# The second attention with transposed scores, three rotating pairs of score banks, and one unit weighed per slot

## The chip, the cores and the metric

The kernel runs on one core of a Trainium2 chip, in one launch. The metric is the time of that launch on the device, in microseconds; the median of three runs is given. Profiled executions are compared by their span, from the first to the last instruction of the core.

## The reference, cut to what matters

The kernel computes two layers in a row on an image batch of 2 x 256 channels x 32 x 32, in fp32. The first is a deformable attention with a bias network and an MLP; nothing in it is recomputed otherwise by the change. The second is plain self-attention over 1024 positions with 8 heads of 32 channels:

```python
xf = transpose(x.reshape(B, C, N), (0, 2, 1))          # B=2, C=256, N=1024
qkv = (xf @ W_qkv + b_qkv).reshape(B, N, 8, 96)
q, k, v = split(qkv, 3, axis=-1)
attn = einsum('bihd,bjhd->bijh', q, k) * 32 ** -0.5
attn = softmax(attn, axis=2)                           # over j, the keys
res = einsum('bijh,bjhd->bihd', attn, v).reshape(B, N, 256)
x = transpose(res @ W_out + b_out + xf)                # back to B, C, 32, 32
```

There are 16 pairs of batch and head (G), and the kernel calls each a head.

## The kernel before, in words

Five engines run written-out instruction orders and wait for one another by counting semaphores. SP issues nearly all DMAs, in order. Up to the end of the first layer's MLP (about 1026 us) the change touches only where some small tiles lie and one wait of SP.

**V, Q and K.** TensorE first computes V for 16 blocks of 128 positions (L1026: two products of 128x256 each, fp32), and VectorE adds the bias (L741). Then eight units compute Q and K, alternately, for 128 channels x 1024 positions (L1038: four products of 128x512). An fp32 product shows in the profile as two records. ScalarE writes the high part in fp32r (L531), VectorE the remainder (L767), and SP stores both to DRAM (`q_d`, `k_d`, L299). Between these, VectorE splits V into three bf16 parts.

**The attention loop.** A head's Q and K come back from DRAM as a stack: four copies of 32 rows, high and low parts paired so that one fp32r product of 128 rows sums high x high, high x low, low x high and low x low. Each of 16 heads has 8 units of 128 queries. For a unit, TensorE makes the scores 128 queries x 1024 keys in two matmuls (L1047). VectorE reduces them to the negated maximum (L773), ScalarE takes the exponential with it as bias (L535), and TensorE turns the result in eight 128x128 transposes (L1055). The turned probabilities are split into fp16 high and low parts: ScalarE copies out of PSUM (L540, L543), VectorE casts and subtracts (L776, L779), GpSimd subtracts the other half (L390). TensorE then weighs them with V in sixteen matmuls of 97 columns (L1063), the 97th being the sum. VectorE inverts the sum (L786), ScalarE scales (L550), and GpSimd adds the three parts (L395, L397). The loop is rolled, two heads in a turn. Two pairs of PSUM banks hold scores, one pair the turned values, one pair the outputs.

**The end.** 32 transposes (L1102) and copies (L574) bring the result to channels x positions, eight units of two 128x512 products apply the output weights (L1113), VectorE adds bias and input (L814), and SP stores (L327).

`bank(i, n)` is n banks of PSUM from bank i; NK = 8; HALF = 512.

## Time and profile before

| | us |
|---|---|
| median of 3 runs (lowest, highest) | 1402.49 (1401.10, 1406.26) |
| the profiled execution's own time | 1401.21 |
| its span | 1399.0 |
| V, Q and K (first L1026 to last L1038) | 1027.1 to 1068.7 |
| attention (first L1047 to last L1063) | 1073.9 to 1375.8 |
| final transposes, products, stores | 1378.3 to 1399.0 |

| engine | busy us of the span | share |
|---|---|---|
| PE (TensorE matmul) | 1302.2 | 93% |
| PEld (its weight loads) | 616.0 | 44% |
| DVE (VectorE) | 921.5 | 66% |
| ACT (ScalarE) | 967.6 | 69% |
| POOL (GpSimd) | 748.9 | 54% |

The shares are averages over stages with different limits; the first attention's bias network alone takes some 760 us. A matmul's recorded length includes its way through the array, so matmuls overlap in the records, and the distance from start to start tells more than the length. "Idle before" of a group is what its engine waited ahead of it.

### The profile page before, as it was taken

The page shows a single profiled execution, that of the slowest core. Times are in us where ns is not written, and L with a number is a line of the kernel's source. Part 1 is how long each engine was busy: PE and PEld are TensorE (multiplying, and loading weights), DVE is VectorE, ACT ScalarE, POOL GpSimd, SP SyncE. Part 2 cuts the span into 40 slices and gives each one's busy share as a digit, 9 for nine tenths or more (in the row PEclk, how much of TensorE's full clock was granted, in tenths as well). Part 3 has the DMA queues.
Part 4 walks back from the last instruction along what each step waited for, and adds up shares of the span by engine and source line. Part 5 has one row for each costly group of instructions (what it writes and reads, how often), then busy time and mean ns, then how long its engine had stood idle before and what let it go on. Part 6 is the DMA issues. An engine that isn't in the chain of part 4 may idle for free.

```text
span 1399.0 us, 29958 instructions
## 1 busy us (share of the span) xinstructions
PE 1302.2 (93%) x11666; PEld 616.0 (44%) x11666; DVE 921.5 (66%) x1270; ACT 967.6 (69%) x1263; POOL 748.9 (54%) x681
## 2 busy tenths in 40 slices
PE   3169999999999999999999998799997999999998
PEld 2132222222222222222222226444454888888885
DVE  6876666666666666666666657410037999999995
ACT  3377777777777777777777773332204999999994
POOL 4166666666666666666666652200000767777772
PEclk9579999999999999999999999999999999999999
DMA  2141110111011101110111000000007222212211
GB/s 69 54 134 31 31 32 2 31 31 32 2 31 32 29 4 32 31 26 7 31 32 23 9 1 1 1 0 0 0 29 272 62 60 60 54 45 52 60 30 60
DMA packets 19922, 53.27 MB, mean 38 GB/s; under 512 B 4642, under 2 KB 7330, under 8 KB 19668
## 3 DMA queue, kind: packets, MB, share of 16 engines
q1 hardware_dynamic: 19824, 51.92, 14.1%
q8 instruction: 70, 1.15, 0.4%
q14 instruction: 24, 0.20, 0.0%
q10 hardware_dynamic: 4, 0.01, 0.0%
HBM read 40.95 MB, written 10.95 MB: 37 GB/s over the span
## 4 chain that ended last, share of the span: by engine, by line
PE 80%; DVE 11%; issue 3%; ACT 2%; POOL 2%; DMA 1%; SPq 1%; DVEq 0%; ACTq 0%; POOLq 0%
PE ps L898 31%; PE ps L907 17%; PE ps L889 5%; DVE aneg L773 5%; PE ps L1055 4%; PE ps L1063 4%; PE ps L1004 4%; PE ps L1014 4%; PE ps L1047 3%; DVE conv L620 2%; PE ps L1038 1%; DVE big L776 1%; POOL big L355 1%; PE ps L1026 1%; PE ps L991 1%
## 5 line engine op out<-in xcount | busy, mean ns | idle before, releaser
L898 PE MATMUL ps<-big,w 64*64 64x512 f32 x4096 | 483.5, 589 | 0.0
L479 ACT ACTIVATE big<-ps 128x1024 f32<-128x1024 f32 x256 | 262.0, 1023 | 179.0 <-PE ps L898 179.0
L674 DVE TENSOR_SCALAR big<-big 128x1024 f32<-128x1024 f32 x256 | 177.8, 694 | 263.8 <-POOL big L370 263.8
L668 DVE TENSOR_TENSOR big<-qpad,ps 128x1024 f32<-128x1024 f32 x256 | 311.0, 1215 | 7.8 <-ACT ps L458 5.4
L370 POOL TENSOR_TENSOR big<-qpad 128x1024 f32<-128x1024 f32 x128 | 244.5, 1910 | 133.2 <-PE ps L898 68.6
L370 POOL TENSOR_TENSOR big<-qpad,V 128x1024 f32<-128x1024 f32 x128 | 244.5, 1910 | 129.7 <-PE ps L898 73.5
L479 ACT ACTIVATE big<-ps,vec 128x1024 f32<-128x1024 f32 x256 | 284.0, 1109 | 0.0
L390 POOL TENSOR_TENSOR big<-BT,big 128x512 f16<-128x512 f32 x129 | 150.4, 1166 | 248.0 <-DVE big L776 248.0
L907 PE MATMUL ps<-big,w3s 128*32 128x512 f32 x2048 | 246.2, 598 | 1.3 <-ACT big L479 1.3
L898 PEld LDWEIGHTS ps<-big,w 64*64 64x64 f32 x4096 | 146.6, 133 | 205.9 <-issue 112.6
L773 DVE TENSOR_REDUCE aneg<-ps 128x1 f32<-128x1024 f32 x131 | 158.3, 1209 | 6.0 <-PE ps L1047 5.7
L535 ACT ACTIVATE big<-ps,aneg 128x1024 f32<-128x1024 f32 x130 | 148.5, 1142 | 6.0 <-DVE aneg L773 5.3
L1055 PE MATMUL ps<-ident,big 128*128 128x128 f32 x1032 | 136.3, 274 | 3.8 <-DVE big L779 3.8
L907 PEld LDWEIGHTS ps<-big,w3s 128*32 128x32 f32 x2048 | 53.5, 109 | 181.7 <-ACT big L479 92.2
L1055 PEld LDWEIGHTS ps<-ident,big 128*128 128x128 f32 x1032 | 121.1, 141 | 23.2 <-DVE big L779 5.7
L1063 PE MATMUL ps<-BT,big 128*128 x2048 | 115.6, 208 | 1.1
L1063 PEld LDWEIGHTS ps<-BT,big 128*128 128x128 f16 x2048 | 99.0, 97 | 21.3 <-issue 10.3
L889 PE MATMUL ps<-S,wl 57*64 57x512 bf16 x1024 | 102.3, 389 | 1.5 <-ACT vs L474 1.5
L1047 PE MATMUL ps<-h1l,h1h 128*128 128x512 f32 x262 | 94.5, 443 | 6.8 <-DMA h1l<-k_d 5.2
L889 PEld LDWEIGHTS ps<-S,wl 57*64 57x64 bf16 x1024 | 29.5, 105 | 144.7 <-ACT big L479 80.7
L779 DVE SCALAR_TENSOR_TENSOR big<-ps,big 128x512 f16<-128x512 f32 x129 | 89.1, 691 | 0.8 <-ACT big L543 0.4
L540 ACT ACTIVATE BT<-ps 128x512 f32<-128x512 f32 x129 | 79.1, 613 | 4.0 <-PE ps L1055 4.0
(140 smaller groups left out, 1116.5 us busy)
## 6 DMA issues: line engine op xcount, KB each, us to landing
raw<-s_f SPq DMA_DIRECT2D x32, 512.0 KB, 6.1
h1h<-q_d SPq DMA_DIRECT2D x64, 128.0 KB, 3.0
h1l<-k_d SPq DMA_DIRECT2D x64, 128.0 KB, 3.1
q_d<-XN SPq DMA_DIRECT2D x8, 512.0 KB, 2.6
k_d<-XN SPq DMA_DIRECT2D x8, 512.0 KB, 2.6
X<-in_x SPq DMA_DIRECT2D x2, 1024.0 KB, 6.3
out<-X SPq DMA_DIRECT2D x8, 256.0 KB, 2.0
m<-grid_d SPq DMA_DIRECT2D x1, 1024.0 KB, 4.6
```

The costliest lines, as they stand in the source:

```text
L370: pool.tensor_tensor(h1[m % HRING].rearrange("p (y a b) -> p y a b", y=2, b=W), u.unsqueeze(2).to_broadcast(shape), a[:, :, HALF // W * hf ...
L390: pool.tensor_tensor(PTL[u % 2][:, 0:HALF], PF[u % 2], PTH[u % 2][:, 0:HALF], ALU.subtract).then_inc(pFl_ready, 1)
L479: act.activation(h2[m % H2RING], z2[m % ZRING], ACT.Relu, bias=v("cb2") if m % 2 else 0.0).then_inc(h2_ready, 1)
L535: act.activation(PR[u % 2], bank(2 * (u % 2), 2), ACT.Exp, bias=aneg[u % 2][:, :]).then_inc(pr_ready, 1)
L668: dve.tensor_tensor(h1[m % HRING].rearrange("p (y a b) -> p y a b", y=2, b=W), u.unsqueeze(2).to_broadcast(shape), b[:, :, HALF // W * hf: ...
L674: dve.tensor_scalar(h1[m % HRING], h1[m % HRING], 0.0, None, ALU.max).then_inc(h1_ready, 1)
L773: dve.tensor_reduce(aneg[u % 2][:, :], bank(2 * (u % 2), 2), AX.X, ALU.max, negate=True).then_inc(mx_ready, 1)
L889: pe.matmul(z2[m % ZRING][CH * y:CH * (y + 1), HALF * x:HALF * (x + 1)], wl1[CH * x:CH * x + KROWS, 2 * w + y, :], S[CH * x:CH * x + KROWS ...
L898: last = pe.matmul(z2[m % ZRING][CH * y:CH * (y + 1), HALF * x:HALF * (x + 1)], w2[CH * x:CH * (x + 1), :], h1[m % HRING][CH * x:CH * (x + ...
L907: last = pe.matmul(zb[32 * k:32 * (k + 1), :], w3s[:, a:a + 32], h2[(m + k // 2) % H2RING][:, HALF * (k % 2):HALF * (k % 2 + 1)], start=(m ...
L1055: last = pe.transpose(bank(4 + hf)[:, P * i:P * (i + 1)], PR[u % 2][:, P * jt:P * (jt + 1)], ident[:, :])
L1063: last = pe.matmul(bank(6 + u % 2)[:, 0:VW], pT[u % 2][:, P * jt:P * (jt + 1)], V3[:, 2 * k + u // NK, jt, :], start=(jt == order[0] and p ...
```

## The change

The second attention is written anew.

- V is computed after Q and K. Its bias comes as a third product, of a row of ones with the bias row, and ScalarE copies V out of PSUM.
- The stack has three copies of 32 rows (96) instead of four. Three heads' stacks are held; the first three are loaded after four of the eight units of Q and K are stored, before the rest is.
- The scores are made twice. `along(x)` makes 128 queries x 1024 keys, for which every eighth query is taken as the stationary operand, so only VectorE reads them, for the maxima (`maxes`). `across(s)` makes 128 keys x 1024 queries, with two more rows: a row pair of ones against the high and low parts of the negated maxima, which subtracts them in the product. ScalarE's exponential writes the probabilities already turned, in fp32.
- The maxima travel from 128 partitions x 8 to two rows of 1024: GpSimd splits them (`max_parts`), SP writes them to DRAM and reads them back (`move_max`).
- A slot has one `along` (13 ahead), one `across`, and one `weigh` of two slots before: four matmuls of 256 queries, V (32 columns) being stationary, in four column tiles. For the sum, GpSimd adds the probabilities of two slots, and every second slot four matmuls with ones (`sums`) add them over the partitions. Outputs and sums are 32 rows per quarter of the queries.
- Once per head VectorE inverts the sums and multiplies (`divide`), and SP moves the four quarters into place (`place_head`), so that the final transposes go.
- Scores use three pairs of banks in rotation. All loops are unrolled.
- `conv`, `gel`, `qw` and `kw` of the first layer share memory with other tiles now, and SP waits for `k_ready` ahead of the late weights.

```diff
-Q_STACK, K_STACK = [0, 0, 1, 1], [0, 1, 0, 1]
-VW = 3 * D + 1
-PSCALE = 2.0 ** 12
+Q_STACK, K_STACK = [0, 0, 1], [0, 1, 0]
+ROWS = D * len(Q_STACK)
+HEADS3, PRING, AHEAD_MAX = 3, 6, 13
+QUARTER = N // 4
 WS_POOL = 4
-UNITS = 2 * NK
+SLOTS = G * NK
...
+        PT = [big[:, 4 + i, :] for i in range(PRING)]
+        PSUMS = [big[:, 11, :], BT[:, 14:16, :].rearrange("p a b -> p (a b)")]
+        OT = [big[:, 10, QUARTER * i:QUARTER * (i + 1)] for i in range(2)]
+        orec = [big[:, 10, QUARTER * i:QUARTER * (i + 1)] for i in (2, 3)]
...
+        def along_banks(x):
+            return 2 * (x % 2 if x < AHEAD_MAX else 2 * (x - AHEAD_MAX) % 3)
+        def across_banks(s):
+            return 2 * ((2 * s + 1) % 3)
...
+            sp.wait_ge(k_ready, 1)
...
+            def load_head(n):
+                i = n % HEADS3
+                for r in range(len(Q_STACK)):
+                    sp.dma_start(QS[i][D * r:D * (r + 1), :].bitcast(fp32), q_d[Q_STACK[r], D * n:D * (n + 1), :]).then_inc(st_in[i], 16)
+                    sp.dma_start(KS[i][D * r:D * (r + 1), :].bitcast(fp32), k_d[K_STACK[r], D * n:D * (n + 1), :]).then_inc(st_in[i], 16)
+            def move_max(n):
+                sp.wait_ge(m_lo, n + 1)
+                sp.dma_start(m_d[n].rearrange("a (q t) -> q a t", t=NK), mparts[n % HEADS3][:, :, :].bitcast(fp32)).then_inc(m_out, 16)
+                sp.wait_ge(m_out, 16 * (n + 1))
+                sp.dma_start(QS[n % HEADS3][ROWS:ROWS + 2, :].bitcast(fp32), m_d[n]).then_inc(m_in, 16)
+            def place_head(n):
+                sp.wait_ge(o_done, n + 1)
+                row, t = D * (n % HP), n // HP
+                for c in range(4):
+                    sp.dma_start(rT[row:row + D, t, QUARTER * c:QUARTER * (c + 1)], OT[n % 2][D * c:D * (c + 1), :]).then_inc(rT_in[n % 2], 16)
+            for n in range(4):
                 send_parts(n)
             for i in range(2):
-                sp.wait_ge(parts_out[i], 32 * 3)
-            load_head(0, 0)
-            load_head(1, 1)
-            for n in range(6, 2 * T):
+                sp.wait_ge(parts_out[i], 32 * 2)
+            for n in range(HEADS3):
+                load_head(n)
+            for n in range(4, 2 * T):
                 send_parts(n)
             for i in range(2):
                 sp.wait_ge(parts_out[i], 32 * T)
-            with sp.Fori(0, G // 2 - 1) as k:
-                sp.wait_ge(sc_ready, UNITS * k + NK)
-                load_head(0, 2 * k + 2)
-                sp.wait_ge(sc_ready, UNITS * k + 2 * NK)
-                load_head(1, 2 * k + 3)
-            sp.wait_ge(sc_ready, UNITS * (G // 2 - 1) + NK)
-            sp.sem_inc(st_in[0], 16 * 2 * HP)
+            for n in range(G):
+                move_max(n)
+                if n >= 2:
+                    place_head(n - 2)
+                if HEADS3 <= n + 2 < G:
+                    sp.wait_ge(st_ready, NK * (n + 2 - HEADS3 + 1))
+                    load_head(n + 2)
+            place_head(G - 2)
+            place_head(G - 1)
...
+            def max_parts(n):
+                pool.wait_ge(mx_ready, NK * (n + 1))
+                if n >= HEADS3:
+                    pool.wait_ge(m_out, 16 * (n - HEADS3 + 1))
+                hi, lo = (mparts[n % HEADS3][:, a, :] for a in range(2))
+                pool.tensor_copy(hi, amax[n % HEADS3][:, :]).then_inc(m_hi, 1)
+                pool.wait_ge(m_hi, n + 1)
+                pool.tensor_tensor(lo, amax[n % HEADS3][:, :], hi.bitcast(fp32), ALU.subtract).then_inc(m_lo, 1)
+            max_parts(0)
+            for j in range(SLOTS // 2):
+                if j % 4 == 1 and j // 4 + 1 < G:
+                    max_parts(j // 4 + 1)
+                pool.wait_ge(pr_ready, 2 * j + 2)
+                if j >= 2:
+                    pool.wait_ge(sums_done, j - 1)
+                pool.tensor_tensor(PSUMS[j % 2], PT[2 * j % PRING], PT[(2 * j + 1) % PRING], ALU.add).then_inc(added, 1)
...
+            for n in range(2 * NK):
+                b, jt = n // NK, n % NK
+                act.wait_ge(vv_ready, n + 1)
+                act.activation(V[:, NH * b:NH * (b + 1), jt, :], bank(4 + n % 4)[:, 0:C].rearrange("p (n d) -> p n d", d=D),
+                               ACT.Identity).then_inc(vv_saved, 1)
+            for s in range(SLOTS):
+                act.wait_ge(st_ready, s + 1)
+                if s >= PRING:
+                    act.wait_ge(pv_done, s - PRING + 1)
+                    act.wait_ge(added, (s - PRING) // 2 + 1)
+                act.activation(PT[s % PRING], bank(across_banks(s), 2), ACT.Exp).then_inc(pr_ready, 1)
...
+            def maxes(x):
+                n, it = x // NK, x % NK
+                dve.wait_ge(sc_ready, x + 1)
+                if it == 0 and n >= HEADS3:
+                    dve.wait_ge(m_lo, n - HEADS3 + 1)
+                dve.tensor_reduce(amax[n % HEADS3][:, it:it + 1], bank(along_banks(x), 2), AX.X, ALU.max, negate=True).then_inc(mx_ready, 1)
+            def divide(n):
+                dve.wait_ge(pv_done, NK * (n + 1))
+                dve.wait_ge(sums_done, NK // 2 * (n + 1))
+                dve.reciprocal(orec[n % 2], bank(6 + n % 2)[:, QUARTER:2 * QUARTER]).then_inc(rec_done, 1)
+                dve.wait_ge(rec_done, n + 1)
+                if n >= 2:
+                    dve.wait_ge(rT_in[n % 2], 64 * (n // 2))
+                dve.tensor_tensor(OT[n % 2], bank(6 + n % 2)[:, 0:QUARTER], orec[n % 2], ALU.mult).then_inc(o_done, 1)
...
+            for x in range(NK):
+                maxes(x)
+            for x in range(NK, SLOTS + 2 * NK + 1):
+                if x < SLOTS:
+                    maxes(x)
+                n = (x - NK - AHEAD_MAX - 3) // NK
+                if n >= 0 and (x - NK - AHEAD_MAX - 3) % NK == 0:
+                    divide(n)
...
+            def value(n):
+                b, jt = n // NK, n % NK
+                if n >= 4:
+                    pe.wait_ge(vv_saved, n - 3)
+                for kt in range(CT):
+                    pe.matmul(bank(4 + n % 4)[:, 0:C], X[:, CT * b + kt, P * jt:P * (jt + 1)], wv[:, kt, 2, :],
+                              start=(kt == 0), stop=False)
+                last = pe.matmul(bank(4 + n % 4)[:, 0:C], one_row[0:1, :], bv[0:1, :, :].rearrange("p n d -> p (n d)"), start=False, stop=True)
+                last.then_inc(vv_ready, 1)
...
+            def along(x):
+                n, it = x // NK, x % NK
+                if it == 0:
+                    pe.wait_ge(st_in[n % HEADS3], 96 * (n // HEADS3 + 1))
+                if AHEAD_MAX + 2 <= x:
+                    pe.wait_ge(pr_ready, x - AHEAD_MAX - 1)
+                elif x >= 2:
+                    pe.wait_ge(mx_ready, x - 1 + (x == AHEAD_MAX))
+                for hf in range(2):
+                    last = pe.matmul(bank(along_banks(x) + hf), QS[n % HEADS3][0:ROWS, it:it + NK * (P - 1) + 1:NK],
+                                     KS[n % HEADS3][0:ROWS, HALF * hf:HALF * (hf + 1)], start=True, stop=True)
                 last.then_inc(sc_ready, 1)
 
+            def across(s):
+                n, kt = s // NK, s % NK
+                if kt == 0:
+                    pe.wait_ge(m_in, 16 * (n + 1))
+                if s - 1 + AHEAD_MAX < SLOTS:
+                    pe.wait_ge(mx_ready, AHEAD_MAX + s - 1 + (s > 0))
+                else:
+                    pe.wait_ge(pr_ready, s - 2)
+                for hf in range(2):
+                    last = pe.matmul(bank(across_banks(s) + hf), KS[n % HEADS3][0:ROWS + 2, P * kt:P * (kt + 1)],
+                                     QS[n % HEADS3][0:ROWS + 2, HALF * hf:HALF * (hf + 1)], start=True, stop=True)
+                last.then_inc(st_ready, 1)
+            def weigh(s):
+                n, kt = s // NK, s % NK
+                if kt == 0 and n >= 2:
+                    pe.wait_ge(o_done, n - 1)
+                pe.wait_ge(pr_ready, s + 1)
+                for c in range(4):
+                    last = pe.matmul(bank(6 + n % 2)[D * c:D * (c + 1), 0:QUARTER], V[:, n, kt, :],
+                                     PT[s % PRING][:, QUARTER * c:QUARTER * (c + 1)],
+                                     start=(kt == 0), stop=(kt == NK - 1), skip_group_check=True)
+                last.then_inc(pv_done, 1)
+            def sums(j):
+                n = j // (NK // 2)
+                pe.wait_ge(added, j + 1)
+                for c in range(4):
+                    last = pe.matmul(bank(6 + n % 2)[D * c:D * (c + 1), QUARTER:2 * QUARTER], ones[:, :],
+                                     PSUMS[j % 2][:, QUARTER * c:QUARTER * (c + 1)],
+                                     start=False, stop=(j % (NK // 2) == NK // 2 - 1), skip_group_check=True)
+                last.then_inc(sums_done, 1)
 
             pe.wait_ge(f_lo, 2 * T)
+            pe.wait_ge(row_ready, 1)
+            for x in range(NK):
+                value(2 * x)
+                value(2 * x + 1)
+                along(x)
+            for x in range(NK, AHEAD_MAX):
+                along(x)
+            pe.wait_ge(vv_saved, 2 * NK)
+            pe.wait_ge(ones_ready, 1 + HEADS3)
+            for s in range(SLOTS + 4):
+                if s + AHEAD_MAX < SLOTS:
+                    along(s + AHEAD_MAX)
+                if s < SLOTS:
+                    across(s)
+                if 0 <= s - 2 < SLOTS:
+                    weigh(s - 2)
+                if s % 2 == 1 and s >= 5:
+                    sums((s - 5) // 2)
+            pe.wait_ge(mx_ready, SLOTS)
+            pe.wait_ge(pr_ready, SLOTS)
...
                 b, ct, hf = n // 4, n // 2 % 2, n % 2
-                pe.wait_ge(rT_saved, 4 * b + 4)
+                if n % 4 == 0:
+                    for i in range(2):
+                        pe.wait_ge(rT_in[i], 32 * NH * (b + 1))
```

## Rows read from the trace of the kernel before

**Rows 1.** The page, part 4: the chain that ended last, by engine

```profile
PE 80%; DVE 11%; issue 3%; ACT 2%; POOL 2%; DMA 1%; SPq 1%; DVEq 0%; ACTq 0%; POOLq 0%
```

**Rows 2.** Stretches: busy us (instructions) of PE, PEld, DVE, ACT, POOL; clock, DMA, GB/s

```profile
1200.00:1300.00 100.00, 98.73 (x1139) 85.37 (x1138) 96.95 (x175) 97.54 (x176) 70.79 (x133) 1.00 0.26 63
```

**Rows 3.** Timeline, one unit of the second attention: start, length, what

```profile
1200.92 0.72 PE L1047 MATMUL ps<-h1l,h1h 128*128 128x512 f32 x2
...
1201.10 1.13 ACT L535 ACTIVATE big<-ps,aneg 128x1024 f32<-128x1024 f32 x1
...
1201.48 1.03 PE L1055 MATMUL ps<-ident,big 128*128 128x128 f32 x8
...
1201.71 1.20 DVE L773 TENSOR_REDUCE aneg<-ps 128x1 f32<-128x1024 f32 x1
...
1203.11 0.71 PE L1047 MATMUL ps<-h1l,h1h 128*128 128x512 f32 x2
```

**Rows 4.** Timeline, the same unit's first score matmul alone

```profile
1200.92 0.48 PE L1047 MATMUL ps<-h1l,h1h 128*128 128x512 f32 x1
```

**Rows 5.** Timeline of TensorE in the bias network, one core, column tiles in between

```profile
96.93 1.92 PE L907 MATMUL ps<-big,w3s 128*32 128x512 f32 x16
98.78 0.41 PE L889 MATMUL ps<-S,wl 57*64 57x512 bf16 x4
99.02 1.89 PE L898 MATMUL ps<-big,w 64*64 64x512 f32 x16
100.74 0.39 PE L889 MATMUL ps<-S,wl 57*64 57x512 bf16 x4
100.96 1.89 PE L898 MATMUL ps<-big,w 64*64 64x512 f32 x16
102.78 1.92 PE L907 MATMUL ps<-big,w3s 128*32 128x512 f32 x16
```

**Rows 6.** Groups by line and shape: count, busy us, mean ns of one, idle before

```profile
L370 POOL TENSOR_TENSOR big<-qpad 128x1024 f32<-128x1024 f32 x128 | 244.5, 1910 | 133.2 <-PE ps L898 68.6 <-DVE big L674 60.0 <-PE ps L868 4.7
...
L907 PEld LDWEIGHTS ps<-big,w3s 128*32 128x32 f32 x2048 | 53.5, 109 | 181.7 <-ACT big L479 92.2 <-issue 89.5
...
L1047 PEld LDWEIGHTS ps<-h1l,h1h 128*128 128x128 f32 x262 | 40.3, 194 | 8.9 <-issue 6.0 <-ACT big L535 2.3
...
L786 DVE RECIPROCAL arec<-ps 128x1 f32<-128x1 f32 x128 | 20.2, 158 | 0.0
...
L741 DVE TENSOR_TENSOR big<-ps,bv 128x256 f32<-128x256 f32 x16 | 6.8, 425 | 7.8 <-PE ps L1026 7.8
...
L713 DVE RECIPROCAL srec<-ssum 128x8 f32<-128x8 f32 x16 | 3.1, 196 | 0.0
...
L634 DVE TENSOR_SCALAR BT<-BT 32x2048 f32<-32x2048 f32 x1 | 1.2, 1214 | 0.0
...
L618 DVE TENSOR_SCALAR conv<-qpad,vec 128x288 f32<-128x288 f32 x1 | 0.5, 500 | 0.0
```

**Rows 7.** The chain that ended last, 1026 to 1110 us: start, length, what

```profile
1027.11 14.08 PE ps L1026 x64
1041.19 20.61 PE ps L1038 x48
...
1064.29 2.63 DMA k_d<-XN
1067.37 0.42 SPq L304
...
1070.15 3.60 DMA h1l<-k_d
```

**Rows 8.** Stretch after TensorE's idle time, columns as in rows 2

```profile
1073.90:1080.00 6.10, 4.49 (x13) 3.28 (x14) 3.56 (x3) 2.58 (x3) 0.00 (x0) 0.50 1.03 284
```

**Rows 9.** The chain that ended last, from 1378 us

```profile
1382.04 13.75 PE ps L1113 x32
```

**Rows 10.** DMA issues: count, KB each, median us from issue to landing

```profile
ident<-in_ident SPq DMA_DIRECT2D x1, 64.0 KB, 6.9
```

More of the change, by code:

```diff
@@ L79, in build @@
         k_d = dram("k_d", [2, G * D, N], fp32)
+        m_d = dram("m_d", [G, 2, N], fp32)
         vec = sb("vec", [P, NVEC])
@@ L99, in build @@
         sc = sb("sc", [P, 4])
-        conv = sb("conv", [P, T * 9, KD])
-        gel = sb("gel", [P, T * 9, KD])
         pwl = sb("pwl", [P, T, 2, G])
@@ L124, in build @@
         vs = sb("vs", [P, T, 2, 2 * D])
+        conv, gel = (big[:, i, 0:T * 9 * KD].rearrange("p (a b) -> p a b", b=KD) for i in (10, 11))
         gb = m1[:, :, :]
@@ L208, in build @@
         rT = XN
-        PR = [big[:, 8, :], big[:, 9, :]]
-        PTH = [big[:, 10, HALF * i:HALF * (i + 1)].bitcast(fp16) for i in range(2)]
-        PTL = [big[:, 11, HALF * i:HALF * (i + 1)].bitcast(fp16) for i in range(2)]
-        PF = [BT[:, 14 + i, :] for i in range(2)]
+        qk3 = sb("qk3", [P, 2, N], fp32r)
         part = [[XN[:, 2 * i + a, :].bitcast(fp32r) for a in range(2)] for i in range(2)]
-        QS = [h1h[:, 2 * i:2 * i + 2, :].rearrange("p a b -> p (a b)") for i in range(2)]
@@ new lines, in build @@
+        PT = [big[:, 4 + i, :] for i in range(PRING)]
+        PSUMS = [big[:, 11, :], BT[:, 14:16, :].rearrange("p a b -> p (a b)")]
+        OT = [big[:, 10, QUARTER * i:QUARTER * (i + 1)] for i in range(2)]
+        orec = [big[:, 10, QUARTER * i:QUARTER * (i + 1)] for i in (2, 3)]
+        amax = [sb(f"amax{i}", [P, NK]) for i in range(HEADS3)]
+        mparts = [sb(f"mparts{i}", [P, 2, NK], fp32r) for i in range(HEADS3)]
+        ones = sb("ones", [P, D])
+        one_row = sb("one_row", [1, P])
@@ L399, in _ @@
[L399 to L410 removed]
+            pool.memset(one_row[:, :], 1.0).then_inc(row_ready, 1)
@@ L1020, in _ @@
             wv = wqkv[:, :, :].rearrange("p t (k n) -> p t k n", k=3)
-            for n in range(2 * NK):
-                b, jt = n // NK, n % NK
-                if n >= 4:
-                    pe.wait_ge(vv_saved, n - 3)
-                for kt in range(CT):
-                    last = pe.matmul(bank(4 + n % 4)[:, 0:C], X[:, CT * b + kt, P * jt:P * (jt + 1)], wv[:, kt, 2, :],
-                                     start=(kt == 0), stop=(kt == CT - 1))
-                last.then_inc(vv_ready, 1)
             pe.wait_ge(qw_scaled, 2)
@@ L1040, in _ @@
                 last.then_inc(p_ready, 1)
-            def scores(u):
-                i, it = u // NK % 2, u % NK
-                for jh in range(2):
-                    last = pe.matmul(bank(2 * (u % 2) + jh), QS[i][:, P * it:P * (it + 1)], KS[i][:, HALF * jh:HALF * (jh + 1)],
-                                     start=True, stop=True)
-                last.then_inc(sc_ready, 1)
-            def turn(u, hf):
-                for i in range(4):
-                    jt = 4 * hf + i
-                    last = pe.transpose(bank(4 + hf)[:, P * i:P * (i + 1)], PR[u % 2][:, P * jt:P * (jt + 1)], ident[:, :])
-                last.then_inc(pT_ready, 1)
@@ L1058, in weigh @@
-            def weigh(u, k):
-                order = list(range(4, NK)) + list(range(4))
-                for jt in order:
-                    for pT in (PTH, PTL):
-                        last = pe.matmul(bank(6 + u % 2)[:, 0:VW], pT[u % 2][:, P * jt:P * (jt + 1)],
-                                         V3[:, 2 * k + u // NK, jt, :],
-                                         start=(jt == order[0] and pT is PTH), stop=(jt == order[-1] and pT is PTL))
-                last.then_inc(oo_ready, 1)
```

188 lines of the change are left out of this document (18 added, 170 removed).

## Prediction

> **What bounds the kernel now.** I read the page's chain of waits first: 80% of the chain that ended last runs through TensorE [rows 1]. The part before 1027 us is untouched by the change, so only 1027 to 1399 us counts, 372 us. The stretch view of the second attention [rows 2] shows TensorE, VectorE and ScalarE all at 97% or more and GpSimd at 71%: three engines tie. Its 176 ScalarE instructions, four for each unit, make 44 units in 100 us, 2.27 each. One undisturbed unit [rows 3] goes from score matmul to score matmul in 2.19 us: 0.56 for two score matmuls, the other 1.63 for eight transposes and sixteen fp16 products. The VectorE reduce inside it takes 1.20. So a gain needs relief on all three engines, and the question is which of them is then the longest.
>
> **What the change does to each engine, per slot of 128 keys.** ScalarE keeps one exponential of 1.13 us [rows 3] and loses two copies and the scaling. VectorE keeps the reduce, which in sequence costs about 1.12 to 1.20, and loses the cast and the fp16 remainder; a divide comes once per head. GpSimd adds two 128x1024 tiles for two slots: 1.91 us [rows 6], 0.96 per slot. TensorE loses transposes and fp16 products but makes the scores twice. It becomes the longest, as follows.
>
> **TensorE per slot.** (a) The four fp32r score matmuls (two along, two across). The first of a pair ends 0.48 after its start [rows 4], both 0.72 after it [rows 3]: 0.24 apart. The pair takes 0.56 to the next instruction, of which 0.09 is the first weight load (I read it as what the first lasts longer than the later ones, 0.48 against about 0.39). So 0.235 each, 0.94. (b) That first exposed load, 0.09. (c) weigh: four column tiles of 128x32. A burst of layer 3 with four rounds of four tiles, 512 columns, lasts 1.85 us [rows 5], 0.43 a round with 0.14 left over; weigh has 256 columns and two rounds, 0.43. (d) sums: the same size for every second slot, 0.215. (e) Going from whole-array to column tiles and back. The same sixteen records take 1.72 us when the next instruction keeps its 64x64 tiles (99.02 to 100.74) and 1.82 when 128x32 tiles follow (100.96 to 102.78); the way back costs 0.14 [rows 5]. Together 0.24 per slot. Sum so far 1.915.
> (f) along takes its stationary columns 8 elements (32 bytes) apart. No TensorE row does that. Bounds: nothing below (the load hides), and above the ratio of VectorE's reads 16 bytes apart: 500 ns for 288 elements against 1214 for 2048 contiguous [rows 6]; less some 0.15 us fixed, 1.22 ns against 0.52, a factor 2.35. A load of 128 columns lasts 0.19, one of 32 columns 0.11 [rows 6]; the difference, 0.085 for 96 columns, makes 0.11 for 128, so the top is +0.145 each. I take 1.22 ns per column as it stands, 156 ns instead of 110: +0.05 for each of two loads, both exposed since the load already fills the gap between such matmuls. **P = 2.01 us** per slot, between 1.91 and 2.20; 1.80 in even slots, 2.23 in odd ones.
> The engines behind: across(s) needs the maximum of along(s+12), issued 1.9 us or more before; reduce plus hand-over is 1.5. Hidden. The exponentials lag by two slots before anyone needs them, the sums' additions by 1.5 slots more. If this cover went, the three pairs of banks would allow about 3.8 us (0.65 along, 1.25 maximum, 0.65 across, 1.2 exponential) for three slots, 1.27 each.
>
> **The divide.** Once a head VectorE runs a reciprocal of 128x256 and a product, between two reduces. Reciprocals: 158 ns for one column, 196 for eight [rows 6]. The slope is 5.4 ns per element; if I set against it the same fixed 0.13 to 0.15 us as for other small operations it is 6 to 8. For 256 columns 1.5 to 2.3 us; I take 2.2. The product is 0.42, as the V bias on 128x256 from PSUM [rows 6]. So 2.7 with a hand-over. It starts when the head's last sums are done, 2.45 us into an odd slot I (2.23 and latency); it ends at 5.15, the next reduce, whose scores have been waiting, at 6.4. across of slot I+2 wants that maximum at 2.23+1.80+0.80 = 4.83. TensorE stands still 1.57 us. Divides 0 to 12 still have reduces behind them: 13 x 1.57 = **20.4 us**. Queued behind that wait are the exponential of the slot and, in TensorE's order, weigh; they follow 1.6 us later and nobody catches up.
> The Trainium skill, "VectorE: DVE Perf Modes" (First, the fixed hardware budget), says reciprocal iterates with a repeat count of 8. By this, at 8 times the reduce's 1.1 ns per element, the operation takes about 2.4 us, and the stalls would be 23 us in all instead of 20; the 196 ns for eight columns agree, if its fixed part is 0.13.
>
> **Prologue.** V moves behind the Q and K projections: 14.08 us go from here [rows 7]. A projection unit is 8 records of 0.43, 3.43 us; the store after unit 5 starts at 1064.29 [rows 7]; two units and 13.9 us earlier is unit 3, at 1043.5, landed 2.6 later, 1046.1. Now SP issues 18 loads before units 4 and 5 are sent: 0.46 each (six between 1067.37 and 1070.15), 8.3 us, to 1054.5. ScalarE may start unit 6 only when store 4 has landed: 1057.6. Then 1.1 and 1.3 for each of units 6 and 7: f_lo 7 at 1061.4, against 1057.2 without this wait. There TensorE starts values. Each has a third product now (one row by 256 columns): 3 x 0.44 = 1.32, sixteen make 21.1; eight pairs of along 4.6; and TensorE has stood idle 7 us, and after an idle of 5 us before, the granted clock was 0.50, its lower level of 1.2 GHz, for 6 us [rows 8], so +2.6: 28.3 us, to 1089.7. Whether the one-row product changes the tiling is not shown: 0 to 3.8 us, I take 0. along 8 to 12 then go at the reduce's pace: six reduces, 7.2, and 0.8 for along 13; across 0 at 1097.7. The first maxima's way through DRAM (0.6 on GpSimd, two DMAs of about 2.7) ends at 1.4+0.6+5.4 = 7.4 of these 8.0.
>
> **The sum.** 114 slots with along x 2.01 = 229.1; minus 2.0 for products that the first slots lack; plus 20.4; 13 slots without along at 0.24+0.09+0.47+0.43+0.215 = 1.445, 18.8. Thus 266.3, across 127 starts at 1364.0 and ends 0.6 later. Tail: exponential 1.35, addition 1.95, sums 0.5, then 13.75 of final products [rows 9] (the transposes are gone, the copies too; the last head's divide 2.7 and four DMAs, 1.4 of issue and 2.3 of landing, end at 10.5, inside the first four units' 10.8), then 3.3 for the last addition and store: 21.1. End at 1385.7, 13.3 before 1399.0. The profiled execution took 1401.2, 2.2 outside its span; its forecast is **1388 us**. The median shown is 1.3 above that execution, which I leave out.
> DMAs that could bite: each head's six loads start when across of the last slot of the freed buffer is done, 0.8 before a slot 8n, and need 5 x 0.46 + 3.6 [rows 7] = 5.9, so land 5.1 into it; along asks at 3 slots, 6.0. Slack 0.9; longer landings would cost 13 times the excess. The late-weights load now waits for k_ready, in a stretch where SP waits for ScalarE anyway: 0.
>
> **Rivals.**
> *A, every strided column of the weights costs double.* along's two loads take 0.11 more each instead of 0.05, P is 2.13, the stall shrinks to 1.35: 114 x 0.12 - 3 + 1 for the prologue, **1399**, no change. With VectorE's factor 2.35, P is 2.20 and the time 1407. For it: the VectorE rows. Against: 512 moving columns pass in 0.235, 2.2 per ns, and weights only at 1.2 per ns, so they may have room. 0.22. The Trainium skill, "SBUF — State Buffer" (Door 1: The DMA port swizzle, note on cachelines), states the penalty: each access that crosses to a new line pays, and fp32 strides are free up to 4 elements; here it is 8.
> *B, the divide does not stall, or weight loads and tile changes hide.* If the reciprocal ran at about 1 ns per element the divide would be 0.8 and end with the next scores: minus 20, **1368**. Hidden loads (P 1.91) give 1378. Against it is the difference of the two reciprocals; 0.20 for both, down to 1358.
> *C, the maxima's round trip is late, slower.* Place: TensorE's wait before slot 0 of each head. From m_lo (2.95 us into slot 2) to that wait are 6 slots, 0.75 and one stall, less 2.95: 11.4 us. It decides from two landings of over 5.2 us. For it: the first DMA writes 256 pieces of 32 bytes, which no row shows, and a 64 KB load once took 6.9 [rows 10]. Two of those make 14.7: 3.3 x 15 heads = 50, **1438**. Against: that load shared the queues with the input; 2.6 is usual. 0.08.
>
> **How the numbers follow.** Forecast 0.45, its own range 1377 to 1400; A 0.22; B 0.20; C 0.08; 0.05 for others, half each way. Faster by over 0.5% (about what a measurement of this kernel can tell from no change) means below 1395.5: 0.34 + 0.20 + 0.03 = 0.57. Slower, above 1409.5: C, a third of A, and others: 0.19, and I allow 0.22 for loads above A's. Same: 0.21. The range leaves out C and the deep end of B: 1360 to 1414.
>
> **What would show it.** TensorE's pitch in the second attention near 2.0 us with an idle gap of about 1.6 before the across matmul five slots into each head, released by a VectorE reduce; a reciprocal row of 2.0 to 2.3 us; the two along matmuls further apart than 0.24, or not (A, B); a wait on POOL or the DMA of m_d in front of across (C); ScalarE at about 55%. It is wrong if the pitch is under 1.8 or over 2.25, if the reciprocal is below 1 us, or if the prologue up to across 0 ends away from 1098 by more than 4.

## The result: slower, 1429.9 us

The changed kernel takes 1429.92 us, the median of four runs (1424.60 to 1432.33); the kernel before, with four runs, 1404.38. The ratio is 1.0179 with a 95% interval of 1.014 to 1.0217. The forecast was 1388, with a range of 1360 to 1414. Spans of the profiled executions: 1399.0 before, 1422.8 after, 23.8 more.

The page of the changed kernel: span, busy times, slices of the span (TensorE, granted clock).

```profile
span 1422.8 us, 24717 instructions
...
PE 1312.7 (92%) x10372; PEld 520.6 (37%) x10372; DVE 801.0 (56%) x889; ACT 810.4 (57%) x883; POOL 699.3 (49%) x396
...
PE   3169999999999999999999998899969999999998
...
PEclk8579999999999999999999999999985599999999
```

The slices carry the finding. TensorE is full, as before, but its clock shows 8, 5, 5 and 9 tenths in slices 30 to 33, where the page before shows 9 throughout; for two slices of 35.6 us it runs at half its clock. In these slices V, and the first `along`, are made.

The way there, on the chain that ended last (start, length, what), 1040 to 1068 us:

```profile
1044.63 2.62 DMA k_d<-XN
...
1047.31 0.32 SPq L311
...
1055.57 0.42 SPq L306
...
1056.03 6.11 DMA q_d<-XN
...
1067.18 1.22 PE ps L994 x2
```

The landings of the stores of Q and K (L306) issued from 1055 us on:

```profile
DMA to landing us min/median/max: 2.6/5.4/7.3
```

The store after unit 3 lands at 1047.25 and 18 head loads follow, to 1055.5, as worked out (1046.1 to 1054.5). The store of unit 4 then takes 6.11 us to land, not 2.6: it stands behind the loads, and the first stretch below shows the DMA engines full (share 1.02). The store of unit 5, next in the queue, is the 7.3 us one and lands at 1064.59; ScalarE's part of unit 7, which needs its buffer free, starts at 1064.70. TensorE waits 11.3 us in all and starts V at 1067.18.

The stretches of the idle time, of V with `along` 0 to 7, and of slots in the steady part (columns as in rows 2 of the kernel before):

```profile
1057.00:1062.00 5.00, 0.00 (x0) 0.00 (x0) 0.00 (x0) 0.00 (x0) 0.00 (x0) 0.65 1.02 343
1067.00:1125.00 58.00, 57.82 (x113) 32.84 (x114) 8.70 (x8) 6.87 (x17) 0.00 (x0) 0.50 0.04 17
1140.00:1240.00 100.00, 95.48 (x736) 52.77 (x736) 66.44 (x57) 47.18 (x47) 56.71 (x35) 1.00 0.24 56
```

For 58 us TensorE is busy with hardly a gap (57.82 of 58.00) and the granted clock stays at 0.50, the 1.2 GHz level; by the trace it is there from 1058.5 to 1137.0. The kernel before got back to 1.00 after less than 7 us that were less busy, 4.49 of 6.10 [rows 8]; the stretch after those rows, of the kernel before:

```profile
1080.00:1090.00 10.00, 9.46 (x106) 8.17 (x105) 9.05 (x17) 9.34 (x16) 5.57 (x8) 0.98 0.27 111
```

Now the steady part, where the first exponential is at 1134.8 and the last at 1401.4. First an even slot, from one `along` pair (L1009) over `across` (L1023) and `weigh` to the next pair, with VectorE's reduce in between:

```profile
1249.71 0.88 PE L1009 MATMUL ps<-qk 96*128 96x512 f32 x2
...
1250.43 0.63 PE L1023 MATMUL ps<-h1h,h1l 98*128 98x512 f32 x2
1250.63 1.23 DVE L737 TENSOR_REDUCE amax<-ps 128x1 f32<-128x1024 f32 x1 [1.51 <-PE ps L1009]
...
1251.56 0.88 PE L1009 MATMUL ps<-qk 96*128 96x512 f32 x2
```

Then, from 1255.68, an odd slot with `sums` (L1044):

```profile
1255.68 0.88 PE L1009 MATMUL ps<-qk 96*128 96x512 f32 x2
1256.39 0.62 PE L1023 MATMUL ps<-h1h,h1l 98*128 98x512 f32 x2
1256.94 0.64 PE L1034 MATMUL ps<-big 128*32 128x256 f32 x8
1257.40 0.61 PE L1044 MATMUL ps<-big,ones 128*32 128x256 f32 x8
1257.94 0.88 PE L1009 MATMUL ps<-qk 96*128 96x512 f32 x2
```

From `along` to `along` it is 2.26 us in the odd slot (1255.68 to 1257.94) and 1.85 in this even one (1249.71 to 1251.56; others 1.84); the unit of rows 3 took 2.19 for as many scores. The forms that answer to rows 6 (count, busy us, mean ns of one), and the three waits of TensorE after 1020 us that matter here:

```profile
L433 POOL TENSOR_TENSOR BT<-big 128x1024 f32<-128x1024 f32 x32 | 76.1, 2379 | 44.0 <-ACT big L567 44.0
...
L1009 PEld LDWEIGHTS ps<-h1l,h1h 96*128 96x128 f32 x176 | 49.4, 327 | 40.7 <-issue 36.9 <-DVE amax L737 3.2
...
L1023 PEld LDWEIGHTS ps<-h1h,h1l 98*128 98x128 f32 x176 | 32.9, 195 | 18.1 <-DVE amax L737 11.6 <-issue 3.3
...
L743 DVE RECIPROCAL big<-ps 128x256 f32<-128x256 f32 x16 | 28.1, 1758 | 22.5 <-PE ps L1044 22.5
```

```profile
PE ps L1023 <- DVE amax L737: 12.0, 14, 0.9
PE ps L994 <- DVE XN L754: 11.3, 1, 11.3
...
PE ps L1044 <- POOL BT L433: 1.3, 1, 1.3
```

One weight load of `along` takes 0.33 us against 0.19 of `across`; the reciprocal takes 1.76 us, the product after it 0.42 as taken. GpSimd's addition takes 2.38 us, not 1.91, and stays hidden but for one wait of 1.3 us. (The row of 1.91 reads repeated elements by `to_broadcast`, this addition plain ones; whether that is the cause isn't tested.) The 12.0 us are stalls of `across` for a maximum behind a divide: the time between two exponentials, sorted by its place in the head, is 3.00 us in one place of eight (heads 3 to 12, 2.99 to 3.01) where the other even slots have 1.83 to 1.85. A head takes 17.6 us; the unit of before, 2.30 us over the whole loop (1076.4 to 1373.6 for 129 steps), makes 18.4.

### The profile page after: what moved, and what is told of

The parts are those of the page before. It is cut to its first block, busy times and chain, and to the rows that moved or that the text cites. A ratio compares the mean times of both kernels' runs of the same rounds, so it can differ in the third digit from the quotient of the medians.

```text
span 1422.8 us, 24717 instructions
## 1 busy us (share of the span) xinstructions
PE 1312.7 (92%) x10372; PEld 520.6 (37%) x10372; DVE 801.0 (56%) x889; ACT 810.4 (57%) x883; POOL 699.3 (49%) x396
## 4 chain that ended last, share of the span: by engine, by line
PE 86%; DVE 7%; POOL 2%; ACT 1%; DMA 1%; issue 1%; SPq 1%; POOLq 0%; DVEq 0%; ACTq 0%
PE ps L853 31%; PE ps L862 17%; PE ps L1009 6%; PE ps L844 5%; PE ps L1034 4%; PE ps L1023 4%; PE ps L959 4%; PE ps L969 4%; PE ps L994 2%; DVE big L613 2%; PE ps L1044 2%; DVE big L743 2%; DVE amax L737 1%; PE ps L996 1%; POOL big L379 1%; PE ps L984 1%
## 5 line engine op out<-in xcount | busy, mean ns | idle before, releaser
L502 ACT ACTIVATE big<-ps 128x1024 f32<-128x1024 f32 x256 | 261.9, 1023 | 178.9 <-PE ps L853 178.9
L502 ACT ACTIVATE big<-ps,vec 128x1024 f32<-128x1024 f32 x256 | 284.0, 1110 | 0.0
L737 DVE TENSOR_REDUCE amax<-ps 128x1 f32<-128x1024 f32 x128 | 155.1, 1222 | 128.9 <-PE ps L1009 128.9
L567 ACT ACTIVATE big<-ps 128x1024 f32<-128x1024 f32 x128 | 131.0, 1023 | 145.9 <-PE ps L1023 145.9
L422 POOL CAST mparts<-amax 128x8 fp32r<-128x8 f32 x16 | 3.0, 188 | 225.9 <-DVE amax L737 225.9
L433 POOL TENSOR_TENSOR big<-big 128x1024 f32<-128x1024 f32 x32 | 76.1, 2379 | 75.6 <-ACT big L567 75.6
L433 POOL TENSOR_TENSOR BT<-big 128x1024 f32<-128x1024 f32 x32 | 76.1, 2379 | 44.0 <-ACT big L567 44.0
L1009 PE MATMUL ps<-h1l,h1h 96*128 96x512 f32 x176 | 81.6, 551 | 2.1 <-DVE amax L737 2.1
L1034 PE MATMUL ps<-big 128*32 128x256 f32 x1024 | 81.6, 391 | 0.0
L1023 PE MATMUL ps<-h1h,h1l 98*128 98x512 f32 x176 | 57.8, 410 | 8.1 <-DVE amax L737 8.1
L729 DVE SCALAR_TENSOR_TENSOR X<-ps,vec,X 128x512 f32<-128x512 f32 x8 | 6.0, 751 | 105.0 <-PE ps L969 105.0
L1009 PEld LDWEIGHTS ps<-h1l,h1h 96*128 96x128 f32 x176 | 49.4, 327 | 40.7 <-issue 36.9
```

The lines of the kernel that those rows point to most:

```text
L433: pool.tensor_tensor(PSUMS[j % 2], PT[2 * j % PRING], PT[(2 * j + 1) % PRING], ALU.add).then_inc(added, 1)
L502: act.activation(h2[m % H2RING], z2[m % ZRING], ACT.Relu, bias=v("cb2") if m % 2 else 0.0).then_inc(h2_ready, 1)
L567: act.activation(PT[s % PRING], bank(across_banks(s), 2), ACT.Exp).then_inc(pr_ready, 1)
L737: dve.tensor_reduce(amax[n % HEADS3][:, it:it + 1], bank(along_banks(x), 2), AX.X, ALU.max, negate=True).then_inc(mx_ready, 1)
L1009: last = pe.matmul(bank(along_banks(x) + hf), QS[n % HEADS3][0:ROWS, it:it + NK * (P - 1) + 1:NK], KS[n % HEADS3][0:ROWS, HALF * hf:HALF * ...
L1034: last = pe.matmul(bank(6 + n % 2)[D * c:D * (c + 1), 0:QUARTER], V[:, n, kt, :], PT[s % PRING][:, QUARTER * c:QUARTER * (c + 1)], start=( ...
```

## The experiments

Two theories after the result. **R**: once the clock is down, the one-row products of V (1 x 256, L996), a third of its TensorE time, keep it down. **I**: the idle of 11 us ahead is the cause, whatever follows. And beside them, what each of the other terms costs. The experiments up to e7, and e9 and e11, are one run each; the four runs of the changed kernel lie within 8 us.

### e1: the bias product on 128 rows

```diff
-                last = pe.matmul(bank(4 + n % 4)[:, 0:C], one_row[0:1, :], bv[0:1, :, :]..., start=False, stop=True)
+                last = pe.matmul(bank(4 + n % 4)[:, 0:C], one_row[:, :], bv[:, :, :]..., start=False, stop=True)   # one_row: [P, P] of 1/P
```

> The V bias product uses 128 rows of 1/128 against the bias on all partitions instead of one row of ones: as many products, columns and microseconds of TensorE, but full height and no change of tile shape. Theory R (the one-row products keep the clock at its lower level once it has fallen): the granted clock is back at 1.00 within about 6 us of the first value product, as in [rows 8]; V and the first eight along take about 30 us instead of 58, the time falls by 25 to 30 us, to about 1395 to 1400. Theory I (the idle of 11 us before it is the cause, whatever follows): the stage stays at 0.50 and within 2 us of its 58, the time within 4 us of the changed kernel's 1425 to 1432.

Measured: 1393.03 us in one run, span 1391.2, 31.6 less than the changed kernel. The stage's stretches:

```profile
1067.00:1071.00 4.00, 4.00 (x10) 3.20 (x10) 0.00 (x0) 0.38 (x1) 0.00 (x0) 0.50 0.48 192
1071.00:1096.00 25.00, 24.12 (x107) 21.15 (x106) 10.77 (x9) 7.03 (x16) 0.39 (x2) 1.00 0.00 1
```

The idle before is unchanged (11.1 us), and after 4 us the clock is back. The first exponential comes at 1103.2 instead of 1134.8; the last follows it by 266.6 us here and 266.7 there. Theory I falls: the idle alone doesn't make the 58 us. By this single run the kernel is ahead of the one before, which had 1402.1 on the same chip.

### e2: no third product at all

```diff
-                last = pe.matmul(bank(4 + n % 4)[:, 0:C], one_row[0:1, :], bv[0:1, :, :]..., start=False, stop=True)
```

> Leaves out the third product of each value (the bias of V in the second attention). Theory R: the clock recovers within about 6 us, V and the first eight along take 16 x 0.88 + 8 x 0.65 + 3 = 22 us instead of 58, time about 36 us less. Theory I: the stage stays at 0.50 and only loses its sixteen third products at 1.15 us each, 18 us less.

This kernel leaves out the bias of V. Measured: 1390.39 us, span 1388.6, 34.2 less, as R said. The clock was at 1.00 from 1075.3 on, 4.3 us after the start of the values. Against e1 it gains only 2.6 us; its values started at 1071.1 instead of 1066.7, so the two are not a clean price for the product.

### e3: no idle before the values

```diff
-            for n in range(4):
+            for n in range(2 * T):
                 send_parts(n)
...
+            for n in range(2 * NK):
+                value(n)
+            pe.wait_ge(f_lo, 2 * T)
+            for x in range(AHEAD_MAX):
+                along(x)
```

> Keeps the one-row product, but takes the idle time before it away: SP stores all eight units of Q and K before it loads heads, and TensorE computes all sixteen values directly behind the projections, then along 0 to 12. TensorE enters the values at the upper clock. Theory I: it stays at 1.00 through the values, which take 16 x 1.32 = 21 us (plus up to 4 for tile changes). Theory R in its strong form: the one-row products pull the clock down within the stage, and the rest of the values runs at 0.50, 35 to 40 us for the stage. A weak form of R (they don't pull it down, but don't let it rise) cannot be told from I here; e1 tells them apart. The thirteen along come one after the other at 1.2 us, 8 us more than when between the values.

Measured: 1413.75 us, span 1412.0. Stretches of the values, the first `along`, the slots from the first `weigh` on, and those after them:

```profile
1057.00:1080.00 23.00, 23.00 (x83) 13.31 (x84) 1.28 (x1) 5.62 (x15) 0.00 (x0) 1.00 0.58 153
1080.00:1087.00 7.00, 6.17 (x19) 3.56 (x17) 3.18 (x3) 2.05 (x3) 0.00 (x0) 0.88 0.00 0
1106.00:1160.00 54.00, 54.00 (x248) 25.22 (x244) 21.07 (x19) 16.32 (x16) 20.23 (x13) 0.50 0.14 33
1162.00:1200.00 38.00, 36.20 (x286) 19.79 (x284) 26.08 (x22) 17.60 (x18) 21.03 (x13) 1.00 0.21 51
```

The one-row products don't pull a high clock down: 23 us at 1.00. But the `along` at the pace of the reduce leave gaps, the clock falls at 1085.4, and then the steady slots themselves, busy for 54.00 of 54.00 us, stay at 0.50 until 1160.4. The first three heads take 23.4, 27.7 and 20.4 us instead of 17.6. So it isn't the one-row product alone that can hold the clock down.

### e4: contiguous weights for `along`

```diff
-                    last = pe.matmul(..., QS[n % HEADS3][0:ROWS, it:it + NK * (P - 1) + 1:NK],
+                    last = pe.matmul(..., QS[n % HEADS3][0:ROWS, P * it:P * (it + 1)],
```

> along takes 128 neighbouring queries as its stationary operand instead of every eighth; the maxima subtracted then belong to other queries. It prices the strided weight load in the steady part, where the changed kernel's slots take 1.84 and 2.27 us. Theory S (a column 32 bytes on costs double, 328 against 194 ns a load): both loads of along get 0.13 shorter and both are exposed, so a slot falls by 0.20 to 0.26, to about 1.62 and 2.05, except that the stall of a head grows by about as much as two slots shrink: 17.6 us for a head become about 16.3. Rival: other parts of TensorE's order take their place, less than 0.05 a slot.

Measured: 1418.98 us, span 1417.2 (its V stage at 0.50, as in the changed kernel). `along`'s loads after 1150 us:

```profile
L1009 PEld LDWEIGHTS ps<-h1l,h1h 96*128 96x128 f32 x144 | 21.9, 192 | 30.4 <-issue 28.8 <-ACT big L567 1.6
```

This kernel subtracts the maxima of other queries. The load falls from 0.33 to 0.19 as theory S said, 0.14 each, but a slot only from 1.84 to 1.70 and from 2.27 to 2.13: about one of the two loads' excess is paid. The slot with the stall grows from 3.00 to 3.14 while the others shrink, and a head takes 16.76. Two heads took 18.3: in each the clock went to 0.50 once, at 1313.8 and 1365.0, after a stall, and came back at 1317.2 and 1368.4.

### e7, e9, e11: what in the one-row product holds the clock

```diff
 e7   one_row[0:D, :], bv[0:D, :, :]        # 32 rows of 1/32
 e9   for n in range(4 * m, 4 * m + 4): one-row product, start=True
      for n in range(4 * m, 4 * m + 4): two full products
      along(2 * m); along(2 * m + 1)
 e11  one_row[:, :], bv[:, :, :]            # [P, P], row 0 of ones, 127 rows of zeros
```

> The changed kernel with the bias product on 32 rows of 1/32 instead of one row (still a change of tile height each way, as with one row). Theory R1 (few rows in a third of the products hold the clock down): it recovers partly or wholly, since 32 rows work; the stage near e1's 28 to 35 us. Theory R2 (the change between tile heights holds it down, however many rows work): the stage stays at 0.50 and 58 us as with one row. Either way the tile change itself shows: a third product a value of 0.43 plus about 0.1 each way at the upper clock.

> The changed kernel with the same sixteen one-row products, but in groups: four bias products, then the eight full products of the same four values, then two along. A quarter of the changes of tile height, the same one-row time. Theory R2 (the changes between tile heights hold the clock at its lower level): the clock recovers in the V stage, within about 6 us of its start, and the time falls by 20 to 30 us from 1425. Theory R1 (a third of the products' time with few rows in use holds it down): the stage stays at 0.50, within 3 us of 58.

> The bias product on 128 rows of which only the first holds ones and the other 127 zeros: full height and no tile change, as e1 (1391 us of span, clock back after 4 us of values), but with no work in 127 rows. If the tile's height counts, it behaves as e1. If the numbers that flow count (zeros are as good as no rows), it stays at 0.50 as the changed kernel, 58 us for the stage and a span of some 1422.

Measured, one run each: e7 1424.49 us (span 1422.7), e9 1396.35 (1394.6), e11 1393.97 (1392.2). First e7's stretch, then two of e9 and its two groups of TensorE:

```profile
1067.00:1125.00 58.00, 57.85 (x113) 32.87 (x114) 8.67 (x8) 6.90 (x17) 0.00 (x0) 0.50 0.04 17
```

```profile
1067.00:1070.00 3.00, 3.00 (x8) 2.08 (x7) 0.00 (x0) 0.00 (x0) 0.00 (x0) 0.50 0.61 246
1070.00:1080.00 10.00, 10.00 (x35) 7.91 (x35) 2.35 (x2) 1.67 (x5) 0.00 (x0) 0.80 0.00 0
```

```profile
1066.60 3.77 PE L993 MATMUL ps<-bv,one_row 1*128 1x256 f32 x8 [11.37 <-DVE XN L754]
1070.30 5.57 PE L997 MATMUL ps<-qpad,X 128*128 128x256 f32 x16
```

32 rows are as bad as one, to 0.1 us in the span. 127 rows of zeros are as good as e1: the height of the tile that the instruction takes counts, not the numbers. And e9, with the same one-row products in groups of four, gets its clock back at 1074.1 (the 0.80 over 1070 to 1080), while sixteen full-height records (5.6 us, from 1070.30) run without a change. So R1, the share of such products, falls. What stays is that short alternation of tile heights held the clock down; whether it is the number of changes or the length of the unbroken stretches between them, e9 doesn't tell, since it alters both. Nor do the runs tell whether a change acts by itself or by a short standstill of the array, which the busy time of a trace would not show.

### e5 and e6: the prologue's order, the divide

```diff
 e5, beside e1:
+            load_head(0)
             for n in range(4, 2 * T):
                 send_parts(n)
+            for n in range(1, HEADS3):
+                load_head(n)
...
+            for n in range(4):
+                value(n)
+            pe.wait_ge(f_lo, 2 * T)
+            for x in range(AHEAD_MAX):
+                along(x)
+                if x < 2 * NK - 4:
+                    value(4 + x)
 e6, beside e1:
+            for x in range(NK, SLOTS + 2 * NK + 4):
...
+                n, p = divmod(x - NK - AHEAD_MAX - 3, NK)
+                if n >= 0 and p < 4:
+                    divide(n, p)                  # 64 of the 256 columns
```

> e1 (128-row bias product) with another prologue order: SP loads only the first head between the stores of the Q and K units 3 and 4; TensorE computes four values before it waits for the remainders, and then one value behind each of the along 0 to 11. Theory: e1 still loses 10 us of TensorE idle before the values, 3 us of lower clock behind it, and the idle between along 8 and 12 lets the clock fall again for some 8 us. With TensorE busy throughout, the first exponential of the second attention comes at 1085 to 1088 us instead of 1103, and the clock stays at 1.00: 15 to 22 us less than e1's 1393. Rival: the store of unit 4 still waits on the loads ahead of it in the shared DMA engines (6 us landing as before), so that the idle stays: under 8 us less.

> e1 with the head's divide in four pieces of 64 columns, one behind each of four reduces. In e1 the slot pitch is 1.84 and 2.27 us, with one of 3.00 a head: a stall of 1.16. Theory D (the reciprocal of 1.76 us between two reduces holds the maximum that across waits for): the slot of 3.00 falls to 1.84 and none of the next three grows by more than 0.1, a head goes from 17.6 to 16.45, 13 x 1.16 = 15 us less than e1's 1393. Rival: the pieces with their fixed 0.15 and a hand-over each (0.85 a piece) only spread the stall: a head above 17.0, under 8 us less.

Measured: e5 1385.09 us (span 1383.3), 7.9 less than e1; e6 1388.34 (1386.5), 4.7 less. Both fell short, each for a reason in its trace. e5's first exponential comes at 1086.5, as expected, but then the clock falls in a gap before slot 0 and the first slots run at 0.50 until 1110: its first head takes 23.7 us, not 14.8. A stretch of these slots:

```profile
1090.00:1108.00 18.00, 18.00 (x86) 8.08 (x85) 6.66 (x6) 6.14 (x6) 6.98 (x5) 0.50 0.05 12
```

The traces also show where the clock was when the slots began to alternate, that is at the first `weigh` (a product in column tiles). In eight of them (the changed kernel, e1, e2, e4, e6, e7, e9, e11) it had risen from 0.50 some 0.6 to 1.2 us before the first `weigh`, behind `along` and `across` alone, which change only between 96 and 98 rows; in e12, below, it rose 1.1 us after it. In e3 and e5 the first `weigh` came at 0.50, at 1105.8 and 1090.1, and the clock took another 54.6 and 20.0 us. That fits the reading of e9; it is an observation, no run varied it alone.

e6's slot of 3.00 is gone (1.83), but another, two slots earlier in the head, grew from 1.83 to between 2.59 and 2.93; a head takes 17.3. TensorE's waits after 1100 us, and SP's own rows ahead of one of them:

```profile
PE ps L1015 <- DMA h1l<-k_d: 6.6, 8, 1.0
PE ps L1015 <- DMA qk<-k_d: 2.9, 4, 0.8
```

```profile
1253.05 2.42 SPq L326 DMA_DIRECT2D XN<-big  x4
1255.51 0.59 SPq L311 DMA_DIRECT2D qk<-q_d  x1
```

`place_head` stands ahead of `load_head` in SP's queue and waits for the end of the divide, which four pieces moved back; the six loads start only when it is through, and `along` of the next head waits for K. So most of the stall was turned into a new wait.

### e8, e10, e12: together

> 128-row bias product, the prologue order of e5 and the divide in quarters: all three findings together. If the three are independent, 1430 - 31 (clock in the V stage) - 18 (order) - 15 (stall) = 1365 us, between 1355 and 1375, ratio to the kernel before 0.965 to 0.98. If the clock can also be lost in the steady slots (as e3 showed for 60 us after the along had run with gaps), it lands above 1380 in some runs.

e8 (e5 and e6 in one): 1372.75 us (1370.63 to 1388.60), ratio 0.9799 (0.9732 to 0.9867). The run of 1388.60 had a mean clock of 0.961, the others 0.974 to 0.976; where it lost its clock no trace shows.

```diff
 e10, beside e8:
                 move_max(n)
+                if HEADS3 <= n + 2 < G:
+                    sp.wait_ge(st_ready, NK * (n + 2 - HEADS3 + 1))
+                    load_head(n + 2)
                 if n >= 2:
                     place_head(n - 2)
```

> e8 (1371 to 1375 with one run at 1389; a head 17.25 us) with SP loading the next head before it places the one finished. In e8 TensorE waits 0.8 us a head for the load of K, which SP issued only after place_head had waited for the divide, now 4 slots later. Theory: that wait goes, a head takes 16.4 to 16.5 us and 12 heads give 9 to 10 us: 1361 to 1365. Rival: the load still lands late by itself (it can start only when across of slot 8n-1 is done): a head above 17, less than 3 us gained.

e10: 1361.82 us (1359.46 to 1367.94), ratio to the kernel before 0.9717, interval 0.9687 to 0.9747. A head takes 16.39 to 16.49, and all that TensorE still waits for from 1050 to 1400 us is this; below it the stretch that answers to the 58 us:

```profile
PE ps L1016 <- DVE amax L738: 1.4, 1, 1.4
PE ps L1051 <- POOL BT L434: 1.3, 1, 1.3
PE ps L1030 <- DVE amax L738: 0.6, 2, 0.4
```

```profile
1057.00:1085.00 28.00, 26.59 (x119) 23.74 (x117) 17.77 (x15) 7.97 (x19) 0.39 (x2) 1.00 0.41 118
```

It beats both kernels: the design was good for 42 us, in another order.

> e10 (1359 to 1368) with the one-row bias product of the changed kernel put back; TensorE enters the values at the upper clock and has no gap before the attention's slots. If the one-row products only keep the clock from rising, as e3 says, the stage stays at 1.00 and costs sixteen times two tile changes of about 0.1 more, 3 us: 1362 to 1371. If with along between the values they can also pull it down, the V stage takes some 20 us longer and the time is above 1380.

e12 (e10 with the one-row product): 1371.38 us (1369.40 to 1373.72), 9.6 more, a bit above the expected range. Its values, and the stretches:

```profile
1059.44 1.13 PE L1001 MATMUL ps<-qpad,X 128*128 128x256 f32 x4
1060.50 0.69 PE L1003 MATMUL ps<-bv,one_row 1*128 1x256 f32 x2
1061.13 1.13 PE L1001 MATMUL ps<-qpad,X 128*128 128x256 f32 x4
```

```profile
1055.00:1086.00 31.00, 31.00 (x107) 19.56 (x106) 13.59 (x12) 7.10 (x15) 0.39 (x2) 1.00 0.53 171
1094.00:1098.00 4.00, 3.77 (x9) 2.93 (x10) 2.12 (x3) 1.02 (x1) 0.00 (x0) 0.50 0.00 0
```

From value to value it is 1.69 us (1059.44 to 1061.13) where e10 has 1.29: the two changes of height cost 0.40 a value, where another pair of changes makes 0.24 by [rows 5]; 6.4 in all, above the 3.8 that the prediction had as its bound. What makes up the rest of the 9.6 is not broken down. The stage keeps its 1.00, and the clock is lost only in the gap before slot 0, from 1093.9 to 1100.7. So the 58 us need both: a stage entered at the lower clock, and products that alternate in height.

## Why the prediction was wrong

It foretold 13 us less in the span, and there were 24 more: 37.1 us, of which 36.5 lie before the first exponential (1098.3 in the sum, 1134.8 measured). `across` of slot 0 started at 1133.7, so the prediction's own sign of being wrong, more than 4 us away from 1098, came.

**The step that failed is in the prologue, a term mis-sized because of a wrong mechanism: "28.3 us, to 1089.7" for V and the first `along`, with +2.6 for the clock.** I took the 6 us at the lower level of [rows 8] for the time the clock needs to come back, and applied it to other instructions. Measured: 58 us at 0.50, from 1067.2 to 1125. e1 shows the cause by one edit: 31.6 of the 37.1 us return, and its V with the first eight `along` take 27.1 us (1066.7 to 1093.8), near the 28.3. (That the stage was entered at the lower clock is the other half: e12 entered it at 1.00 and kept it.) The one-row product was named, as a tiling change "not shown: 0 to 3.8 us, I take 0"; its price in time was off too (6.4 in e12), but its effect on the clock was in no case of mine. The row for 6 us had been read without asking what ran in it: only products of full height.

**The second step: the stores that follow the head loads land in 2.6 us.** f_lo 7 came at 1067.1 instead of 1061.4, 5.7 us, which with 31.6 makes 37.3, the 37.1 but for 0.2. Of the 5.7, 1.1 are a later start (1047.2 instead of 1046.1) and 3.5 the landing of store 4, 6.11 us behind 18 loads of 128 KB. The other 1.2 lie in units 6 and 7: the sum has 3.8 us for them, although 1.1 and 1.3 for each make 4.8, and the trace has 5.0, because unit 7 had to wait for store 5, which the prediction left out.

**The steady part was right, in sum better than in its terms.** Between the first and the last exponential I worked out 266.3 us; measured 266.7. The pitch was 2.06, not 2.01: a strided load lasts 0.14 longer, not 0.05 and not rival A's 0.11, but of two such loads e4 shows only 0.14 a slot paid, where the sum had 0.10 and rival A 0.22. The stall was 1.16, not 1.57: the reciprocal took 1.76 us, near the 1.54 that the slope of its two rows gives, and not the 2.2 taken. The two errors, 114 x 0.05 and 13 x 0.41, cancel; that the forecast of this part came out within 0.4 us is luck. (In the tail the written terms add to 20.9, not 21.1; measured, 21.4.)

The Trainium skill, "VectorE: DVE Perf Modes" (First, the fixed hardware budget), gives reciprocal a repeat count of 8, from which the prediction estimated 2.4 us. The trace has 1.76 us, 6.3 ns per element above the one-column row and 5.7 times the 1.1 ns taken for the reduce, and the measurement decides. The Trainium skill, "SBUF — State Buffer" (Door 1: The DMA port swizzle), says that an access which crosses to a new line pays. The trace agrees in kind: with a stride of 32 bytes a load takes 328 ns, against 192 in e4.

**The tile changes in a slot**, 0.24 in the sum, fit, though no run varied them alone: e4's even slot takes 1.70, and the even slot was worked out as 1.80 with 0.10 for the stride, 1.70 without it.

**Rival B** fell: the divide stalls, 1.16 us a head, and the stall is gone only in e10. **Rival C**, the maxima's way: the DMA of 256 pieces lands in 1.5 us in the median, and TensorE's waits name no such DMA.

```profile
m_d<-mparts SPq DMA_DIRECT2D x16, 8.0 KB, 1.5
```

**Head loads**: "slack 0.9" held in the changed kernel, no wait for K is in its list. It went in e6 and e8, where the divide ends later.

## What to carry to other kernels

An idle time of TensorE is to be priced with what follows it. Full-height products gave the clock back in 4 to 7 us here; products that alternate between tile heights, or between whole array and column tiles, ran at half the clock for 58 and 54 us at 100% busy. So keep such a stage from being entered at the lower clock (e12), put unbroken full-height products ahead of it (e9 hints at it, no run tried only that), and make small side products full-height with zeros: e11, one run, costs 0.9 us against e1, no more than runs of one kernel differ.

When a wait is moved back in time, look at what stands behind it in the same queue: the split divide gained 0.3 us a head until SP's loads no longer stood behind its result, and 1.15 then.

## What was not expected of the hardware

- A busy TensorE does not by itself get its clock back: 57.82 of 58.00 us busy, granted clock 0.50 throughout.
- For the clock, a product on 32 rows equals one on a single row (spans of 1422.7 and 1422.8), and 128 rows of which 127 are zero equal 128 of data (1392.2 and 1391.2).
- A one-row product between full ones costs 0.40 us more than one of full height at the upper clock.
- What remains open: whether the number of height changes or the length of the stretches between them decides, whether a change of tile acts by itself or by a standstill that the trace doesn't show, and what ends the low clock of alternating slots after 20 us in e5 and 55 in e3.
